# Second attention of a four-stage gated block: scores for the maxima from a stack of their own, and the value products moved into the middle of a step

## The chip, the cores and the metric

The kernel runs on one core of one Trainium2 chip. The metric is the device time of one execution in microseconds (us). A core has five engines that run side by side and wait for one another through semaphores: TensorE (PE; its weight loads are listed apart as PEld), VectorE (DVE), ScalarE (ACT), GpSimd (POOL) and SyncE (SP), which here only issues transfers (DMAs).

## The reference, cut to what matters

Four sublayers are added to x (4 batches, 1024 tokens, 256 channels) one after the other. The change lies in the third, a cross attention of 16 heads of 16 dimensions over 77 context tokens per batch:

```python
def _L1_xattn_ref(values, keys, queries, mask, Wv, Wk, Wq, Wo, bo):
    ...
    energy = jnp.einsum('bqhd,bkhd->bhqk', q, k)
    energy = jnp.where(mask, energy, jnp.float32(-1e+20))
    attn = jax.nn.softmax(energy / np.sqrt(HEAD), axis=-1)
    out = jnp.einsum('bhqk,bkhd->bqhd', attn, v).reshape(N, Lq, EMBED)
    return out @ Wo.T + bo
...
x = x + jnp.tanh(g_xattn[1]) * _L1_xattn_ref(ctx_1024, ctx_1024, _layernorm(x, axis=-1), mask_1x1xSxS2_bk0, ...)
```

x and ctx_1024 are float32. The mask (1024 x 77) is the same for all batches and heads.

## The kernel before, in words

The program is written out by hand: each engine has its own function, the order of its calls is the order of its instructions, and semaphores tie the engines together. The first attention, the expert layer, the second attention and the last attention follow one another; the second attention takes the stretch from 186 to 348 us.

**Operands.** The float32 queries (the normalised x) and keys are split into bfloat16 parts (high, middle, low) and written to memory outside the core (`x_parts`, `ctx_key_parts`). SP loads them back as *stacks*: for one unit, six groups of 16 rows (`Q_ORDER`, `K_ORDER`), so that one bfloat16 matmul over 96 rows adds up the six products of parts. `load_x_stack` (lines 547 to 555) does this with six transfers of 128 KB per unit, each filling 16 partitions that lie next to one another. Three stacks `Xs` are in use in turn; four more rows (96 to 99) take the row maxima. `K1s` is the same for the keys of all heads and batches.

**Units and steps.** A unit u (of 16) is one batch and four heads; a step m (of 32) is half a unit, 512 tokens. `scores1(m)` on PE (line 1456) goes over the four heads j. For each it first makes one *tile* of the next unit for the maxima, `max_product1`: one mask matmul of 308 columns (line 1438, weights `mb1`, moving operand `I4`, four identities side by side) and four matmuls of 77 columns (line 1440), 128 tokens by four heads by 77 keys. Then it makes the transposed scores of its own head, 77 keys by 512 tokens: line 1473 from the stack with the maxima's rows, line 1474 for the mask. In between, in eight of the steps (m = 4, 6, ... 18; the table `HALVES`), ahead of the third head, it transposes a *half* chunk of the normalised x for a later batch (`transpose_half`, line 1394).

After the four heads PE makes `values1(m - 1)` (line 1482), the four transposes of the maxima `max_transposes1(m + 2)` (line 1453) and `out_transposes1(m - 2)` (line 1491):

```python
            for m in range(2 * UNITS):
                scores1(m)
                if m >= 1:
                    values1(m - 1)
                if m + 2 < 2 * UNITS:
                    max_transposes1(m + 2)
                if m >= 2:
                    out_transposes1(m - 2)
```

**The other engines in a step.** DVE takes the maximum of each of the four tiles (line 2054; `max_transposes1(m + 2)` waits for the fourth), in a step with a half also the residue of the half between the second and the third maximum (line 2022), and at the end `normalise1` (lines 2073, 2076). ACT takes the four exponentials (line 1086), in a step with a half the high part of it between the second and the third (`part_h`, line 1028), then `copy_out1` (line 1072) and `stage_rows1` (line 1066). POOL copies the staged maxima into the four rows of the stack (line 833) and makes the low parts (lines 823, 825). Two banks take the tiles in turn, three the scores. ACT's `part_h` waits for the transposes, the residue for `part_h`, the third maximum stands behind the residue.

**Ahead of it.** DVE makes `mb1`, the mask as 0 or minus 2^66 (line 2031). POOL fills `I4` (line 804) and the ones rows of `K1s` (line 808), scales a bias (line 813) and then makes the layer norm's factors (`ln_rstd`, lines 776 and 778).

## Time and profile before

| | |
|---|---|
| median of 3 runs | 1233.62 us (1229.71 to 1234.7) |
| the profiled execution's own time | 1234.39 us |
| its span | 1232.7 us |
| PE busy in the span | 1159.2 us (94%), 10391 matmuls |
| DVE busy | 973.4 us (79%) |
| ACT busy | 818.0 us (66%) |
| POOL busy | 254.9 us (21%) |
| transfers | 40.3% of 16 engines' span, 100 MB |

The span is what the profiler saw from the first instruction to the last; what lies around it is 1.7 us. "Busy" counts the time in which an engine had an instruction under way; matmuls overlap, so a busy PE is not one at its peak. The profile also names what an idle engine waited for, and follows the chain of work that ended last.

### The profile page before, as it was taken

The numbers are of one execution on the slowest core, as the hardware profiler recorded it, in microseconds if no ns is written. First come the engines' busy times: TensorE is split into PE (matmuls) and PEld (weight loads), VectorE is DVE, ScalarE is ACT, GpSimd is POOL, SyncE is SP. The second block draws the span as 40 slices with busy tenths as digits, with TensorE's granted clock in tenths as the row PEclk, the third lists the DMA queues.
The fourth block names the chain that finished last, engine by engine and source line by source line (L and its number), as shares of the span: only waits on it lengthen the run. The fifth ranks groups of instructions, "written<-read, shape, count | busy, mean of one in ns | idle before, by whom it ended". The sixth has DMA issues, their size and how long they took to land.

```text
span 1232.7 us, 26184 instructions
## 1 busy us (share of the span) xinstructions
PE 1159.2 (94%) x10391; PEld 529.1 (43%) x10391; DVE 973.4 (79%) x1431; ACT 818.0 (66%) x1470; POOL 254.9 (21%) x200
## 2 busy tenths in 40 slices
PE   6888999999998999789999999999999999999997
PEld 3566675555575456333332332322323333333345
DVE  6996587765447758789999999999999999999812
ACT  2334567777733742228888888888888888888871
POOL 3021346655732423630000000100100001001010
PEclk9999999999999999979999999999999999999999
DMA  6000337565300334741544354535543545264023
GB/s 207 25 1 16 34 92 140 103 130 107 50 26 26 123 108 137 141 67 47 98 65 87 80 98 74 96 64 102 88 85 74 102 83 87 60 103 76 12 68 117
DMA packets 89993, 101.73 MB, mean 83 GB/s; under 512 B 22154, under 2 KB 60300, under 8 KB 89872
## 3 DMA queue, kind: packets, MB, share of 16 engines
q1 hardware_dynamic: 89872, 100.06, 40.3%
q8 instruction: 83, 1.36, 0.5%
q14 instruction: 38, 0.31, 0.1%
HBM read 71.47 MB, written 24.33 MB: 78 GB/s over the span
## 4 chain that ended last, share of the span: by engine, by line
PE 58%; DVE 34%; ACT 4%; issue 2%; DMA 1%; SPq 1%; POOL 1%; POOLq 0%; DVEq 0%; ACTq 0%
DVE sm L2283 23%; PE ps L1719 11%; PE ps L1710 9%; PE ps L1697 7%; PE ps L1482 3%; PE ps L1579 2%; PE ps L1473 2%; PE ps L1474 2%; PE ps L1780 2%; PE ps L1538 2%; PE ps L1491 1%; PE ps L1440 1%; PE ps L1438 1%; DVE XN L1842 1%; ACT W L1163 1%
## 5 line engine op out<-in xcount | busy, mean ns | idle before, releaser
L2283 DVE TENSOR_REDUCE sm<-ps 128x1 f32<-128x1024 f32 x512 | 602.0, 1219 | 35.2 <-PE ps L1697 31.2
L1163 ACT ACTIVATE W<-ps 128x512 f32<-128x512 f32 x1024 | 535.0, 603 | 122.0 <-PE ps L1719 119.6
L1719 PE MATMUL ps<-R 99*32 99x512 bf16 x4096 | 317.9, 384 | 0.9
L1710 PE MATMUL ps<-W,R 128*32 128x512 f32 x2048 | 265.6, 594 | 0.0
L1719 PEld LDWEIGHTS ps<-R 99*32 99x32 bf16 x4096 | 85.1, 94 | 203.5 <-ACT W L1163 155.9
L1697 PE MATMUL ps<-R 50*128 50x512 bf16 x512 | 91.2, 392 | 12.2 <-DVE sm L2283 8.0
L1697 PE MATMUL ps<-KM,R 50*128 50x512 bf16 x512 | 88.7, 384 | 5.2 <-DVE sm L2283 0.2
L1086 ACT ACTIVATE R<-ps 77x512 f32<-77x512 f32 x128 | 75.2, 593 | 21.0 <-PE ps L1474 11.7
L904 POOL COPY R<-R 128x512 f32<-128x512 f32 x16 | 9.8, 613 | 373.3 <-PE ps L1710 373.3
L1710 PEld LDWEIGHTS ps<-W,R 128*32 128x32 f32 x2048 | 63.0, 111 | 46.1 <-issue 0.9
L833 POOL COPY R<-R 4x2048 bf16<-4x2048 bf16 x32 | 60.5, 1892 | 57.0 <-ACT R L1066 49.0
L2054 DVE TENSOR_REDUCE small<-ps 128x4 bf16<-128x308 f32 x128 | 57.2, 473 | 13.7 <-PE ps L1440 13.7
L1697 PEld LDWEIGHTS ps<-R 50*128 50x128 bf16 x512 | 23.3, 93 | 98.9 <-issue 58.2
L923 POOL TENSOR_TENSOR R<-R,W 128x512 f32<-128x512 f32 x8 | 10.2, 1278 | 265.5 <-DMA W<-sum_factors 265.5
L1697 PEld LDWEIGHTS ps<-KM,R 50*128 50x128 bf16 x512 | 23.3, 93 | 95.8 <-issue 64.9
L1579 PE MATMUL ps<-R,W 128*128 128x512 f32 x128 | 57.9, 595 | 0.0
L1473 PE MATMUL ps<-R 100*77 100x512 bf16 x128 | 49.0, 383 | 0.0
L1474 PE MATMUL ps<-R 77*77 77x512 bf16 x128 | 48.6, 380 | 0.0
L1842 DVE TENSOR_SCALAR XN<-X,mv,rstd 128x256 f32<-128x256 f32 x128 | 47.0, 434 | 1.0 <-PE ps L1551 0.2
L2073 DVE RECIPROCAL small<-ps 128x16 f32<-128x16 f32 x32 | 8.3, 258 | 42.4 <-PE ps L1491 42.4
L1440 PEld LDWEIGHTS ps<-R 96*128 96x128 bf16 x512 | 33.9, 97 | 12.4
L1440 PE MATMUL ps<-R 96*128 96x77 bf16 x512 | 39.0, 198 | 0.0
(261 smaller groups left out, 1451.9 us busy)
## 6 DMA issues: line engine op xcount, KB each, us to landing
R<-x_parts SPq DMA_DIRECT2D x96, 128.0 KB, 4.9
R<-q_parts SPq DMA_DIRECT2D x192, 64.0 KB
R<-q_parts SPq DMA_DIRECT2D x96, 128.0 KB
R<-k_parts SPq DMA_DIRECT2D x96, 128.0 KB
q_parts<-R SPq DMA_DIRECT2D x24, 256.0 KB, 2.6
k_parts<-R SPq DMA_DIRECT2D x24, 256.0 KB, 2.8
x_parts<-R SPq DMA_DIRECT2D x6, 768.0 KB, 4.1
X<-in_x SPq DMA_DIRECT2D x4, 1024.0 KB, 10.0
```

What stands on the lines that cost most here:

```text
L833: pool.tensor_copy(Xs[m // 2 % 3][SR:SR1, :, 512 * (m % 2):512 * (m % 2) + 512], mrow1[:, m % 2].unsqueeze(1).to_broadcast([4, 4, 512])).t ...
L1086: act.activation(P1[:, m % 2, j, :], score_bank1(n)[0:KX, :], ACT.Exp, scale=0.25).then_inc(s_e1, 1)
L1163: act.activation(PR[:, s % 2, h, :], third_bank("score", 64 * u + n), ACT.Exp, scale=0.25).then_inc(s_sfree, 1)
L1440: mm = pe.matmul(o[:, KX * j:KX * j + KX], Xs[u % 3][0:SR, j, P * q:P * q + P], K1s[0:SR, 4 * hg + j, KX * b:KX * b + KX], start=False, st ...
L1473: pe.matmul(o, K1s[:, 4 * hg + j, KX * b:KX * b + KX], Xs[u % 3][:, j, t], start=True, stop=False)
L1474: pe.matmul(o, I4[:, 0:KX], mb1[:, t], start=False, stop=True).then_inc(s_sc, 1)
L1579: mm = pe.matmul(o[:, 512 * j:512 * j + 512], wqkv[:, i, C * kind + P * j:C * kind + P * j + P], XNT3[:, i, 512 * c:512 * c + 512], start= ...
L1697: mm = pe.matmul(pl[:, 512 * i:512 * i + 512], QMH[j][h][v, P * q:P * q + P], KM[j][v, h, :], start=True, stop=True)
L1710: mm = pe.matmul(bank(7)[32 * h:32 * h + 32, :], VST[j][:, k, h, :], PR[:, s % 2, h, :], start=(k == 0), stop=(k == TB - 1))
L1719: mm = pe.matmul(o[32 * c:32 * c + 32, :], KST[j][0:MAX_ROW + 1, h, t:t + 32], QST[j][0:MAX_ROW + 1, h, 512 * (s // 8):512 * (s // 8) + 51 ...
L1842: ins_ = dve.tensor_scalar(ln_chunk_buf(c)[:, i, :], X[:, 4 * c + i, :], mv[:, 4 * c + i, 0:1], rstd[:, 4 * c + i:4 * c + i + 1], ALU.subt ...
L2283: dve.tensor_reduce(MX[:, half, h, q:q + 1], bank(2 * ((p + 1) % 2), 2), AX, ALU.max).then_inc(s_tfree, 1)
```

## The change

The second attention's maxima get their own stack. `max_stack1(u)` has 125 rows: 77 rows of the mask (`mb1`, the same for each head) and 48 rows of parts (`QM_ORDER`, three products of parts in place of six). `max_keys1(b)` stands against it: 77 rows of identity and 48 rows of the keys' parts. A tile is then four matmuls of 77 columns over 125 rows, without the mask matmul. There are two such stacks in turn; their mask rows are filled by POOL (unit 0, which also makes `mb1` now) and by DVE (units 1 and 13), and stay in place. Three more transfers of 128 KB per unit fill the parts. Rows of all these loads are interleaved: transfer n fills every sixth row from n (stacks of the scores, `K1s`) or every third (maxima). `values1(m - 1)` on PE and `copy_out1(m - 1)` on ACT move from the end of step m to between its second and its third head. The order of SP's loads and part writes changes, and POOL fills the identities of three more batches in steps 1, 3 and 4.

```diff
+        MAXR = KX + 48
+
+        def max_stack1(u):
+            v = R5[0:MAXR, 2048:4096] if u % 2 == 0 else R1[0:MAXR, 6144:8192] if u < 12 else R4[0:MAXR, 2048:4096]
+            return v.bitcast(BF16).rearrange("p (j n) -> p j n", j=4)
+
+        def max_keys1(b):
+            v = R2f[0:MAXR, 7482:8098] if b == 0 else W[0:MAXR, 2048 + 616 * b:2664 + 616 * b]
+            return v.bitcast(BF16).rearrange("p (h n) -> p h n", h=H)
...
-        WRITES = {2: (2, 3), 5: (4,), 7: (5,), 9: (6,), 11: (7,)}
+        WRITES = {2: (2,), 5: (4,), 7: (5,), 9: (6,), 11: (7,)}
...
                 for n, p in enumerate(Q_ORDER):
-                    sp.dma_start(Xs[u % 3][16 * n:16 * n + 16],
+                    sp.dma_start(x_stack(u)[n:SR:6],
                                  XP[p, 64 * hg:64 * hg + 64, S * b:S * b + S]
-                                 .rearrange("(j d) t -> d j t", d=D)).then_inc(s_xs[u % 3], 16)
+                                 .rearrange("(j d) t -> d j t", d=D)).then_inc(s_xs[(u + 1) % 3], 16)
+
+            def load_max_stack1(u):
+                b, hg = u // 4, u % 4
+                if u == 2:
+                    sp.wait_ge(s_mp, 8)
+                if u >= 3:
+                    sp.wait_ge(s_sc, 8 * (u - 2))
+                if u == 13:
+                    sp.wait_ge(s_pl, 2 * NC)
+                for n, p in enumerate(QM_ORDER):
+                    sp.dma_start(max_stack1(u)[KX + n:MAXR:3],
+                                 XP[p, 64 * hg:64 * hg + 64, S * b:S * b + S]
+                                 .rearrange("(j d) t -> d j t", d=D)).then_inc(s_xs[u % 3], 16)
...
+            def preset_max_keys1(b):
+                pool.tensor_copy(max_keys1(b)[0:KX], identB[0:KX, 0:KX].unsqueeze(1).to_broadcast([KX, H, KX])
+                                 ).then_inc(s_v1m, 1)
+
+            preset_max_keys1(0)
+            pool.wait_ge(s_m1, 16)
+            pool.tensor_scalar(mb1, M1u, -1.0, BIG, ALU.add, ALU.mult).then_inc(s_mk1, 1)
+            pool.wait_ge(s_mk1, 1)
+            pool.wait_ge(s_kw, 16)
+            pool.tensor_copy(max_stack1(0)[0:KX], mb1.unsqueeze(1).to_broadcast([KX, 4, S])).then_inc(s_mk1, 1)
             pool.wait_ge(s_w1, 16 * 28)
...
+                if m in (1, 3, 4):
+                    pool.wait_ge(s_dl, NC)
+                    preset_max_keys1((m + 1) // 2 if m < 4 else 3)
...
                     if j == 2 and half_in(m) is not None:
                         part_h(half_in(m), bank(2))
+                    if j == 2 and m >= 1:
+                        copy_out1(m - 1)
...
-                if m >= 1:
-                    copy_out1(m - 1)
                 if m + 2 < 2 * UNITS:
                     stage_rows1(m + 2)
...
                     o = bank(n % 2)[:, 0:4 * KX]
-                    pe.matmul(o, mb1[:, P * q:P * q + P], I4, start=True, stop=False, skip_group_check=True)
                     for j in range(4):
-                        mm = pe.matmul(o[:, KX * j:KX * j + KX], Xs[u % 3][0:SR, j, P * q:P * q + P],
-                                       K1s[0:SR, 4 * hg + j, KX * b:KX * b + KX], start=False, stop=True,
+                        mm = pe.matmul(o[:, KX * j:KX * j + KX], max_stack1(u)[:, j, P * q:P * q + P],
+                                       max_keys1(b)[:, 4 * hg + j, :], start=(j == 0), stop=True,
                                        skip_group_check=True)
...
                     n = 4 * m + j
+                    if j == 2 and m >= 1:
+                        values1(m - 1)
                     if j == 2 and half_in(m) is not None:
                         pe.wait_ge(s_mrs, m + 2)
                         transpose_half(half_in(m), bank(2))
...
                 scores1(m)
-                if m >= 1:
-                    values1(m - 1)
...
-            dve.wait_ge(s_m1, 16)
-            dve.tensor_scalar(mb1, M1u, -1.0, BIG, ALU.add, ALU.mult).then_inc(s_mk1, 1)
+
+            def mask_rows1(u):
+                dve.tensor_copy(max_stack1(u)[0:KX], mb1.unsqueeze(1).to_broadcast([KX, 4, S])).then_inc(s_mk1, 1)
...
             for n in range(4, FIRST):
                 residue(n, bank(n))
+            dve.wait_ge(s_dl, NC)
+            dve.wait_ge(s_mk1, 1)
+            mask_rows1(1)
             maxima1(1)
...
+                if m == 19:
+                    dve.wait_ge(s_pl, 2 * NC)
+                    mask_rows1(13)
```

On PE, from the half's transposes of a step to its end (before; L1394 the transposes, L1438 and L1440 a tile, L1473 and L1474 a score, L1482 the values, L1453 the maxima's transposes, L1491 those of the output):

```order
L1394 MATMUL ps<-identF,XN 128x128 x4
L1438 MATMUL ps<-R 128x308
L1440 MATMUL ps<-R 128x77 x4
L1473 MATMUL ps<-R 77x512
L1474 MATMUL ps<-R 77x512
L1438 MATMUL ps<-R 128x308
L1440 MATMUL ps<-R 128x77 x4
L1473 MATMUL ps<-R 77x512
L1474 MATMUL ps<-R 77x512
L1482 MATMUL ps<-R,W 32x512 x4
L1453 MATMUL ps<-identB,small 4x128 x4
L1491 MATMUL ps<-identF,R 128x128 x4
```

The same stretch in the changed program, beginning at the values (L1557 the values, L1463 the half's transposes, L1511 a tile, L1548 and L1549 a score, L1524 and L1566 the transposes at the end):

```order
L1557 MATMUL ps<-R,W 32x512 x4
L1463 MATMUL ps<-identF,XN 128x128 x4
L1511 MATMUL ps<-R 128x77 x4
L1548 MATMUL ps<-R 77x512
L1549 MATMUL ps<-R 77x512
L1511 MATMUL ps<-R 128x77 x4
L1548 MATMUL ps<-R 77x512
L1549 MATMUL ps<-R 77x512
L1524 MATMUL ps<-identB,small 4x128 x4
L1566 MATMUL ps<-identF,R 128x128 x4
L1511 MATMUL ps<-R 128x77 x4
L1548 MATMUL ps<-R 77x512
```

The values stood between the last score and the maxima's transposes and now stand ahead of the half's transposes; nothing is left between the last score and the maxima's transposes, and the mask matmul is gone from the tile.

On ACT in such a step, before (L1086 exponentials, L1028 the half's high part, L1072 the copy of the output, L1066 the maxima's rows):

```order
L1086 ACTIVATE R<-ps 77x512 x2
L1028 CAST R<-ps 128x512
L1086 ACTIVATE R<-ps 77x512 x2
L1072 COPY R<-ps 128x512
L1066 CAST R<-ps 4x512
```

and in the changed program (L1157, L1097, L1141 and L1135 are the same four):

```order
L1157 ACTIVATE R<-ps 77x512 x2
L1097 CAST R<-ps 128x512
L1141 COPY R<-ps 128x512
L1157 ACTIVATE R<-ps 77x512 x2
L1135 CAST R<-ps 4x512
```

The copy of the output moved ahead of the third exponential.

On POOL ahead of the second attention, before (L804 `I4`, L808 rows of `K1s`, L813 the bias, L776 and L778 the layer norm's factors):

```order
L804 COPY R<-identB 77x308
L808 COPY R<-identB 4x1232 x4
L813 TENSOR_SCALAR bo<-bo,gates 128x256
L776 TENSOR_SCALAR rstd<-mv 128x8
L778 TENSOR_TENSOR rstd<-rstd,mhalf 128x8
```

and in the changed program (L865 identities, L870 `mb1`, L873 the mask rows of unit 0, then L876 the bias and L828, L830 the factors):

```order
L856 COPY R<-identB 77x308
L860 COPY R<-identB 4x1232 x4
L865 COPY R<-identB 77x1232
L870 TENSOR_SCALAR R<-R 77x1024
L873 COPY R<-R 77x4096
L876 TENSOR_SCALAR bo<-bo,gates 128x256
L828 TENSOR_SCALAR rstd<-mv 128x8
L830 TENSOR_TENSOR rstd<-rstd,mhalf 128x8
```

Three instructions now stand between the rows of `K1s` and the bias, ahead of the factors.

## Rows read from the trace of the kernel before

**Rows 1.** Chain that ended last, 193 to 341 us, shares by line.

```profile
by line: PE ps L1482 20.2%; PE ps L1473 18.7%; PE ps L1474 18.5%; PE ps L1440 11.6%; PE ps L1491 11.5%; PE ps L1438 11.3%; PE ps L1453 4.9%; PE ps L1394 2.4%; issue 0.7%; DVE small L2054 0.3%
```

**Rows 2.** Steps 0, 1, 16 and 17: stretch; busy us and instructions of PE, PEld, DVE, ACT, POOL; clock; DMA.

```profile
193.34:196.81 3.47, 3.33 (x35) 1.94 (x33) 2.29 (x6) 2.77 (x5) 3.33 (x3) 1.00 0.49 161
196.81:201.00 4.19, 4.19 (x42) 2.11 (x40) 3.73 (x11) 3.21 (x7) 3.67 (x3) 1.00 0.51 172
270.04:275.13 5.09, 5.09 (x50) 3.08 (x48) 2.92 (x7) 4.01 (x8) 3.37 (x3) 1.00 0.88 136
275.13:279.81 4.68, 4.68 (x47) 2.58 (x45) 2.41 (x6) 3.54 (x7) 2.19 (x2) 1.00 0.10 25
```

**Rows 3.** Timeline of step 16, which has a half: start, us, engine, line, operation.

```profile
270.04 0.30 PE L1438 MATMUL ps<-R 77*128 77x308 bf16 x1
...
270.18 0.30 PE L1440 MATMUL ps<-R 96*128 96x77 bf16 x4
...
270.76 0.29 PE L1438 MATMUL ps<-R 77*128 77x308 bf16 x1
...
271.47 0.60 PE L1394 MATMUL ps<-identF,XN 128*128 128x128 f32 x4
...
272.16 0.57 ACT L1028 CAST R<-ps 128x512 bf16<-128x512 f32 x1
...
272.76 0.69 DVE L2022 TENSOR_TENSOR R<-ps,R 128x512 f32<-128x512 f32 x1 [1.03 <-ACT R L1028]
...
273.37 0.85 DVE L2054 TENSOR_REDUCE small<-ps 128x4 bf16<-128x308 f32 x2
...
273.42 1.07 PE L1482 MATMUL ps<-R,W 77*32 77x512 f32 x8
...
274.28 0.24 PEld L1453 LDWEIGHTS ps<-identB,small 128*4 128x4 bf16 x4 [0.70 <-DVE small L2054]
274.32 0.39 PE L1453 MATMUL ps<-identB,small 128*4 128x128 bf16 x4
```

**Rows 4.** Timeline, end of step 0, which has no values behind its scores.

```profile
195.62 0.30 PE L1440 MATMUL ps<-R 96*128 96x77 bf16 x4
...
195.96 0.48 DVE L2054 TENSOR_REDUCE small<-ps 128x4 bf16<-128x308 f32 x1 [0.23 <-PE ps L1440]
...
196.49 0.39 PE L1453 MATMUL ps<-identB,small 128*4 128x128 bf16 x4
...
196.81 0.30 PE L1438 MATMUL ps<-R 77*128 77x308 bf16 x1
```

**Rows 5.** POOL's timeline ahead of the second attention, and the copies of line 833.

```profile
139.17 5.92 POOL L808 COPY R<-identB 4x1232 bf16<-4x1232 bf16 x4
145.19 2.03 POOL L813 TENSOR_SCALAR bo<-bo,gates 128x256 f32<-128x256 f32 x1
154.39 1.60 POOL L776 TENSOR_SCALAR rstd<-mv 128x8 f32<-128x8 f32 x1 [7.17 <-DVE mv L2008]
...
L833 POOL COPY R<-R 4x2048 bf16<-4x2048 bf16 x32 | 60.5, 1892 | 57.0 <-ACT R L1066 49.0 <-POOL R L825 3.0 <-POOL R L833 2.7
```

**Rows 6.** DVE: a copy of 3072 elements; last maxima ahead of step 0, transposes that follow.

```profile
L1954 DVE CAST R<-small 128x3072 bf16<-128x3072 f32 x1 | 1.8, 1760 | 0.0
...
191.02 0.85 DVE L2054 TENSOR_REDUCE small<-ps 128x4 bf16<-128x308 f32 x2
...
193.03 0.39 PE L1453 MATMUL ps<-identB,small 128*4 128x128 bf16 x4 [0.65 <-DVE small L2054]
```

**Rows 7.** Timeline, the first tile of step 14.

```profile
260.29 0.29 PE L1438 MATMUL ps<-R 77*128 77x308 bf16 x1 [0.93 <-issue]
```

**Rows 8.** Two stretches of loads: columns as in rows 2, last two DMA share and GB/s.

```profile
4.00:16.00 12.00, 5.93 (x11) 3.62 (x12) 6.69 (x33) 0.83 (x2) 2.02 (x3) 1.00 1.09 354
255.00:260.00 5.00, 4.36 (x39) 2.15 (x37) 4.01 (x11) 3.67 (x7) 1.97 (x2) 1.00 0.97 123
```

**Rows 9.** Timeline, the last values, and what they waited for.

```profile
343.48 1.07 PE L1482 MATMUL ps<-R,W 77*32 77x512 f32 x8 [0.21 <-ACT R L1072]
```

More of the change, by code:

```diff
@@ L222, in build_program, with x_stack @@
         xres = R4[:, 2048:4096].rearrange("p (u j n) -> p u j n", u=2, j=2)
-        Xs = [v.bitcast(BF16).rearrange("p (j n) -> p j n", j=4)
-              for v in (R4[0:SR1, 0:2048], R5[0:SR1, 0:2048], R5[0:SR1, 2048:4096])]
+        QM_ORDER, KM_ORDER = (0, 0, 1), (0, 1, 0)
+        def x_stack(u):
+            v = (R4[0:SR1, 0:2048], R5[0:SR1, 0:2048], R1[0:SR1, 4096:6144] if u == 2 else R2f[0:SR1, 0:2048])[u % 3]
+            return v.bitcast(BF16).rearrange("p (j n) -> p j n", j=4)
+        MAXR = KX + 48
+        def max_stack1(u):
+            v = R5[0:MAXR, 2048:4096] if u % 2 == 0 else R1[0:MAXR, 6144:8192] if u < 12 else R4[0:MAXR, 2048:4096]
+            return v.bitcast(BF16).rearrange("p (j n) -> p j n", j=4)
+        def max_keys1(b):
+            v = R2f[0:MAXR, 7482:8098] if b == 0 else W[0:MAXR, 2048 + 616 * b:2664 + 616 * b]
+            return v.bitcast(BF16).rearrange("p (h n) -> p h n", h=H)
         On = R1[:, :].rearrange("p (i c) -> p i c", i=NT)
@@ L264, in build_program, with group_loads @@
         s_x3 = sem("x3_added")
-        STACK_DMAS = 6
+        STACK_DMAS, MAX_DMAS = 6, 3
+        def group_loads(g):
+            return 16 * sum((MAX_DMAS if n < UNITS else 0) + (STACK_DMAS if n else 0) for n in range(g % 3, g + 1, 3))
         FIRST = 8
@@ L538, in _, with load_max_keys1 @@
             sp.dma_start(M1u, ins["mask1T"]).then_inc(s_m1, 16)
+            def load_max_keys1(b):
+                for n, p in enumerate(KM_ORDER):
+                    sp.dma_start(max_keys1(b)[KX + n:MAXR:3],
+                                 KXP[p].rearrange("(h d) n -> d h n", d=D)[:, :, KX * b:KX * b + KX]
+                                 ).then_inc(s_k1s, 16)
+            load_max_keys1(0)
             for n, p in enumerate(K_ORDER):
-                sp.dma_start(K1s[16 * n:16 * n + 16],
+                sp.dma_start(K1s[n:SR:6],
                              KXP[p].rearrange("(h d) n -> d h n", d=D)).then_inc(s_k1s, 16)
@@ L564, in _ @@
             sp.wait_ge(s_kw, 48)
+            load_max_stack1(0)
             load_x_stack(0)
+            sp.wait_ge(s_dl, NC)
+            load_max_stack1(1)
             sp.wait_ge(s_pl, 4)
@@ L573, in _ @@
                     sp.wait_ge(s_pw[1], 16 * (b + 1))
+                if u >= 2:
+                    load_max_stack1(u)
+                if u == 3:
+                    write_parts(3)
                 load_x_stack(u)
+                if u == 3:
+                    sp.wait_ge(s_k1s, 16 * (MAX_DMAS + STACK_DMAS))
+                    for n in range(1, B):
+                        load_max_keys1(n)
                 for c in WRITES.get(u, ()):
@@ L832, in max_rows1 @@
                     pool.wait_ge(s_sc, 4 * (m - 5))
-                pool.tensor_copy(Xs[m // 2 % 3][SR:SR1, :, 512 * (m % 2):512 * (m % 2) + 512],
+                if m == 10:
+                    for n in range(2):
+                        pool.wait_ge(s_pw[n], 32)
+                pool.tensor_copy(x_stack(m // 2)[SR:SR1, :, 512 * (m % 2):512 * (m % 2) + 512],
                                  mrow1[:, m % 2].unsqueeze(1).to_broadcast([4, 4, 512])).then_inc(s_mrc, 1)
@@ L1424, in _ @@
             keep_warm(3, 4)
-            pe.wait_ge(s_k1s, 16 * STACK_DMAS)
-            pe.wait_ge(s_v1m, 8)
-            pe.wait_ge(s_mk1, 1)
+            pe.wait_ge(s_k1s, 16 * (MAX_DMAS + STACK_DMAS))
+            pe.wait_ge(s_v1m, 9)
             pe.wait_ge(s_v1c, 2)
@@ L1431, in max_product1 @@
                 b, hg = u // 4, u % 4
-                pe.wait_ge(s_xs[u % 3], 16 * STACK_DMAS * (u // 3 + 1))
+                pe.wait_ge(s_xs[u % 3], group_loads(u))
+                pe.wait_ge(s_mk1, 4 if u >= 13 else 3 if u >= 1 else 2)
+                if b >= 1:
+                    pe.wait_ge(s_k1s, 16 * (MAX_DMAS * B + STACK_DMAS))
+                    pe.wait_ge(s_v1m, 9 + b)
                 for q in qs:
@@ L1471, in scores1 @@
                     t = slice(512 * q, 512 * q + 512)
-                    pe.matmul(o, K1s[:, 4 * hg + j, KX * b:KX * b + KX], Xs[u % 3][:, j, t], start=True, stop=False)
+                    pe.matmul(o, K1s[:, 4 * hg + j, KX * b:KX * b + KX], x_stack(u)[:, j, t], start=True, stop=False)
                     pe.matmul(o, I4[:, 0:KX], mb1[:, t], start=False, stop=True).then_inc(s_sc, 1)
```

4 lines of the change are left out of this document (3 added, 1 removed).

## The prediction, made before the changed kernel had run

> **What bounds the kernel now.** I read the chain of waits first, over the 148 us of the second attention: nearly all of it is PE, and the mask matmuls (L1438) alone hold 11.3% of it [rows 1]. The windows by step then show PE busy for the whole of a step: 4.68 us in a plain step, 5.09 us in one with a half [rows 2]. So a matmul taken off PE can shorten a step, as long as nothing else is nearly as late. That second limit is read from two timelines.
>
> In step 16 [rows 3] two heads take 1.43 us (270.04 to 271.47), 0.715 each, and the mask matmul is 0.14 of it (270.04 to 270.18), 0.13 where it is not rounded up. From the maxima's transposes to the next step it is 0.81 us (274.32 to 275.13). The plain step is then 4 x 0.715 + 0.81 + the values, so the values cost 1.01 us, and a half's transposes 5.09 - 4.68 = 0.41 us.
>
> The second reading is how late the maxima's transposes may start. They wait for DVE's fourth maximum. Step 0 has no values after its scores, and there this wait shows: from the fourth tile's first 77 column matmul to the transposes it takes 0.87 us (195.62 to 196.49), with the maximum running in between, and 0.32 more to the next step [rows 4]. PE's own work in that time is less: 0.14 + 0.43 = 0.57 us. In all later steps the values stand there and cover the wait. In a step with a half the path is longer: transposes of the half, ACT's high part, DVE's residue, third and fourth maximum, maxima's transposes: 271.47 to 274.28, 2.81 us, and the values end within 0.04 us of it [rows 3]. That chain has no slack even before the change.
>
> **The change, part by part.** All against the profiled execution, 1234.39 us (span 1232.7).
>
> 1. *Mask matmul gone.* 0.13 us per tile, 0.52 per step if PE stays the limit. The stack's 125 rows in place of 96 cost nothing here: the mask matmul over 77 rows and the score over 100 rows take their columns' time alike. A head then costs 0.585 us.
>
> 2. *Values between second and third head.* They no longer cover the maxima. Plain step: the fourth tile starts at 3 x 0.585 + 1.01 = 2.77 us, the transposes 0.87 later, the next step 0.81 later: 4.45 us, against 4.68. The gain is 0.23, not 0.52. Step with a half: its transposes now start after the values, at 2 x 0.585 + 1.01 = 2.18 us instead of 1.43, and the same 2.81 and 0.81 follow: 5.80 us, against 5.09. **It gets 0.71 us longer.** ACT does not change this: E2 and E3 wait behind `part_h` and the copy, but end before the values of the next step need them. POOL is busy for 3.37 of 5.09 us and has room. Steps 2 to 29 hold 20 plain ones (-4.6 us) and 8 with a half (+5.7). Step 0 loses its 3.47 - 0.52; step 1, 4.19 now, becomes 2.77 + 0.87 + 0.32 = 3.96: together -0.8. Sum of the loop: +0.3.
>
> 3. *POOL ahead of the loop.* It gets a copy of 1232 elements, the mask of 1024 and a copy of 4096. By line 808 (5.92 us for four of 1232, so 1.5 each) and line 833 (1.89 us for 2048) these are 1.5, about 2 (the bias' 256 elements took 2.03, so this is loosely known) and 3.8: 7.3 us [rows 5]. POOL is free from 147.2 us until the factors at 154.39, so 0.1 us would be late; at line 808's rate the last copy takes 4.9 us. I take +0.7, with 0 and +4 as ends. Nothing covers it, since PE stands idle until the normalised x comes.
>
> 4. *DVE's mask rows.* A copy of 4096 bfloat16 elements. The nearest row is a copy of 3072 in 1.76 us, so 2.35 us [rows 6]; the ends are 1.2 (twice that rate) and 4.3 (about the rate of a maximum over a bank). The first stands ahead of the maxima that started at 191.02. Those took 2.0 us to the transposes at 193.03, of which 0.25 was waiting for PE's warm matmuls. So +2.1 us. The second, in step 19, ends 1.5 us into the next step, normalise and first maximum follow, and the third tile waits: +0.6 us.
>
> [...]
>
> 5. *Loads.* Nine transfers per unit instead of six. The maxima's stack is now loaded on its own and first, and the scores' stack is needed a unit later. Before, step 14 waited 0.93 us for the first load of batch 2 [rows 7]: I count -0.9. The queue took 0.97 of the engines for 123 GB/s in those loads, while 128 partition loads ran at 354 GB/s [rows 8]. Interleaved rows should lie nearer the second, and I charge nothing for the three more.
>
> [...] No run so far shows interleaved rows here.
>
> 6. *End.* The last values waited for a copy that now comes before them: 0.4 us at 343.48, where PE waited on ACT [rows 9], and 0.2 us in the two steps without maxima: -0.6. The first tiles ahead of the loop are ready sooner: -0.1. The three identity copies in steps 1, 3 and 4 (1.5 us each) lie in POOL's idle time.
>
> Sum: 0.3 + 0.7 + 2.1 + 0.6 - 0.9 - 0.6 - 0.1 = **+2.1 us**, 1236.5 for that execution. The median of the runs shown is 0.8 us lower, so the forecast is **1235.7 us**: no change. A measurement of this kernel can tell 0.5%, 6.2 us, from none: below 1227.5 is faster, above 1239.8 slower.
>
> **Rivals.**
>
> *The maxima are not exposed* (DVE starts or ends earlier than I think, or the half's chain does): then steps fall to PE's own sum, 4.16 and 4.57 us. 20 x -0.52 and 8 x -0.52 in place of -4.6 and +5.7 make the result 15.7 us lower, 1220. PE's full occupation speaks for it, step 0 against it. Chance 0.15.
>
> *Half of that*: plain steps as forecast, but the half's chain is shortened (the high part may begin as soon as the first half's transposes are out): half steps stay at 5.1, the result is 5.7 lower, 1230. Chance 0.15.
>
> *Loads become the limit.* The interleaving gives nothing: a unit's 1152 KB at 123 GB/s are 9.4 us, and 384 KB of parts written 1.1 at the rate of the wide load, 10.5 together, against 10.25 for a unit (4.45 + 5.80). It decides from the moment a unit's loads take longer than its two steps, first at step 14, where the part of a batch is written just before. 0.3 us for each of 12 units and about a microsecond at each of three batches: +6, 1242. The 0.97 share at 123 GB/s speaks for it, the wide load's 354 against it. Chance 0.12.
>
> *The copies are slow.* POOL's 4 us and DVE's 4.3 us twice: +3.3, +2, +2: 1243. It decides once POOL ends after 154.39. Chance 0.1; POOL's 2.03 us for 256 elements speaks for it.
>
> **How the numbers follow.** The forecast as computed has 0.48 and lies between 1232 and 1240. Range: 1226 to 1243; it leaves out most of the first rival and the upper tails, two in ten. Faster: the first rival and a quarter of the second, 0.2. Slower: both last rivals where they pass 1239.8 (0.17) and the edge of the forecast, 0.23. The same: 0.57.
>
> **What would show it.** In the changed trace: a plain step of 4.45 us with PE idle for some 0.3 us ahead of the maxima's transposes, released by the maximum; a half step of 5.8 us with over a microsecond there; no wait at step 14; POOL's factors after 154.4 us; the last maxima ahead of step 0 about 2 us later. Steps of 4.2 and 4.6 us would make it wrong on the fast side; a wait for a load at a unit's first tile on the slow side.

## The result, and the profile after

| | before | changed |
|---|---|---|
| median | 1232.8 us (1229.71 to 1234.7, 4 runs) | 1247.34 us (1242.86 to 1251.2, 4 runs) |
| profiled execution | 1234.39 us, span 1232.7 | 1247.35 us, span 1245.6 |

The changed kernel takes 1.0112 times as long, 95% interval 1.0084 to 1.0139: slower, and above the forecast's range (1226 to 1243). PE makes fewer matmuls (10263, 10391 before), but is busy for as long: 1161.1 us, 1159.2 before. The page of the changed kernel, busy us (share of the span) and instructions:

```profile
PE 1161.1 (93%) x10263; PEld 521.8 (42%) x10263; DVE 977.5 (78%) x1432; ACT 814.1 (65%) x1470; POOL 264.3 (21%) x206
```

Where the 13 us of the two profiled executions lie is read by distances between five marks, the same instructions in both timelines: POOL's first copy for the second attention, DVE's first normalised x, the first and the second of the maxima's transposes, and the last. Timelines of the changed kernel at these marks:

```profile
141.20 0.44 POOL L856 COPY R<-identB 77x308 bf16<-77x308 bf16 x1 [10.37 <-PE ps L1457]
...
163.19 2.67 DVE L1915 TENSOR_SCALAR XN<-X,mv,rstd 128x256 f32<-128x256 f32 x8
...
196.48 0.39 PE L1524 MATMUL ps<-identB,small 128*4 128x128 bf16 x4 [0.57 <-DVE small L2129]
...
202.38 0.58 PE L1524 MATMUL ps<-identB,small 128*4 128x128 bf16 x4 [0.65 <-DVE small L2129]
...
349.87 0.38 PE L1524 MATMUL ps<-identB,small 128*4 128x128 bf16 x4
```

| stretch | before | changed | difference |
|---|---|---|---|
| start to POOL's first copy | 138.67 | 141.20 | +2.5 |
| to the normalised x | 19.11 | 21.99 | +2.9 |
| to the first transposes | 30.99 | 33.29 | +2.3 |
| to the second transposes | 4.26 | 5.89 | +1.6 |
| to the last transposes (loop) | 142.49 | 147.49 | +5.0 |
| to the end | 897.16 | 895.77 | -1.4 |

The last row lies behind the change: over all profiles below that stretch took 894.0 to 899.1 us, so its -1.4 tells nothing.

The steps first. The windows of steps 16 (with a half) and 17 in the changed kernel, columns as in [rows 2]:

```profile
284.25:290.15 5.90, 4.90 (x47) 2.60 (x45) 2.91 (x7) 3.84 (x8) 3.33 (x3) 1.00 0.71 159
290.15:294.69 4.54, 4.41 (x42) 2.12 (x40) 2.41 (x6) 3.35 (x7) 2.22 (x2) 1.00 0.17 59
```

A step with a half went from 5.09 to 5.90 us, a plain one from 4.68 to 4.55 [rows 2]. In the half step PE is idle for a full microsecond. The timeline of step 16 in the changed kernel shows where:

```profile
284.24 0.31 PE L1511 MATMUL ps<-W,R 125*128 125x77 bf16 x4
...
284.83 0.31 PE L1511 MATMUL ps<-W,R 125*128 125x77 bf16 x4
...
285.51 1.06 PE L1557 MATMUL ps<-R,W 77*32 77x512 f32 x8
...
286.51 0.66 PE L1463 MATMUL ps<-identF,XN 128*128 128x128 f32 x4
...
287.20 0.59 ACT L1097 CAST R<-ps 128x512 bf16<-128x512 f32 x1 [0.99 <-PE ps L1463]
...
287.82 0.69 DVE L2095 TENSOR_TENSOR R<-ps,R 128x512 f32<-128x512 f32 x1 [1.89 <-ACT R L1097]
...
288.43 0.85 DVE L2129 TENSOR_REDUCE small<-ps 128x4 bf16<-128x308 f32 x2
...
289.33 0.39 PE L1524 MATMUL ps<-identB,small 128*4 128x128 bf16 x4 [1.00 <-DVE small L2129]
```

The values (L1557) stand ahead of the half's transposes (L1463); from there the chain of ACT, DVE and two maxima takes 289.33 - 286.51 = 2.82 us, as before [rows 3]. It starts later in the step by what the values take. A head takes 0.59 us (284.24 to 284.83).

The two stretches ahead of the loop are DVE's and POOL's. Timelines of the changed kernel, DVE and POOL from 147 to 160 us:

```profile
145.31 1.22 DVE L2067 TENSOR_TENSOR R<-R 128x1024 f32<-128x1024 f32 x1 [3.45 <-ACT R L1083]
147.66 2.30 DVE L2072 SCALAR_TENSOR_TENSOR X<-R,gates,X 128x1024 f32<-128x1024 f32 x1 [1.12 <-ACT R L1087]
149.88 2.05 DVE L2067 TENSOR_TENSOR R<-R 128x1024 f32<-128x1024 f32 x1
153.06 3.41 DVE L2072 SCALAR_TENSOR_TENSOR X<-R,gates,X 128x1024 f32<-128x1024 f32 x1 [1.12 <-ACT R L1087]
...
161.99 1.28 DVE L2072 SCALAR_TENSOR_TENSOR X<-R,gates,X 128x1024 f32<-128x1024 f32 x1 [1.12 <-ACT R L1087]
```

```profile
147.67 1.21 POOL L865 COPY R<-identB 77x1232 bf16<-77x1232 bf16 x1
148.97 1.90 POOL L870 TENSOR_SCALAR R<-R 77x1024 bf16<-77x1024 uint8 x1
150.93 4.46 POOL L873 COPY R<-R 77x4096 bf16<-77x4096 bf16 x1
155.38 1.89 POOL L876 TENSOR_SCALAR bo<-bo,gates 128x256 f32<-128x256 f32 x1
159.91 1.06 POOL L828 TENSOR_SCALAR rstd<-mv 128x8 f32<-128x8 f32 x1 [2.65 <-DVE mv L2081]
```

POOL's own lateness cost nothing: it waited 2.65 us for DVE before the factors. But DVE's operation at L2072 takes 1.28 us alone and 2.30 and 3.41 us beside POOL's copies. The excess is about what is left of POOL's copy when DVE starts: 155.39 - 153.06 = 2.33 us are left, 3.41 - 1.28 = 2.13 came on top. That the copy is the cause, and not only the neighbour in time, is what an experiment below tests.

PE then has nothing to do, and its granted clock falls. Windows of the changed kernel, columns as above:

```profile
160.00:170.00 10.00, 5.34 (x21) 4.53 (x21) 7.75 (x14) 6.06 (x9) 2.64 (x2) 0.72 0.00 0
...
200.00:210.00 10.00, 8.24 (x56) 4.21 (x60) 6.35 (x15) 4.43 (x8) 8.04 (x6) 0.66 0.50 138
```

A mean granted clock of 0.72 and 0.66 means that part of each stretch ran at a lower clock: by windows of 2 us it was 1.00 from 160 to 164 and 0.50 from 166 to 170 us, 0.97 from 200 to 202 and 0.50 from 202 to 208. The timeline shows the idle PE ahead of it, and what runs slowly then (PE and DVE):

```profile
164.72 4.02 PE L1463 MATMUL ps<-identF,XN 128*128 128x128 f32 x16 [4.54 <-DVE XN L1915]
...
198.74 1.84 DVE L2105 COPY R<-R 77x4096 bf16<-77x4096 bf16 x1
...
201.11 0.62 PE L1511 MATMUL ps<-R 125*128 125x77 bf16 x8 [1.90 <-DVE small L2129]
...
205.36 0.63 PE L1548 MATMUL ps<-R 100*77 100x512 bf16 x1
```

The copy L2105 stands ahead of the second maxima, PE waits 1.90 us for them, and a score matmul takes 0.63 us in step 0, where in later steps it takes 0.38. Step 0 took 5.08 us, 3.47 before [rows 2], and forecast at 2.95.

### The profile page after: what moved, and what is told of

Its sections match the earlier page's. It is cut to its first block, busy times and chain, and to the rows that moved or that the text cites. A ratio compares the mean times of both kernels' runs of the same rounds, so it can differ in the third digit from the quotient of the medians.

```text
span 1245.6 us, 26125 instructions
## 1 busy us (share of the span) xinstructions
PE 1161.1 (93%) x10263; PEld 521.8 (42%) x10263; DVE 977.5 (78%) x1432; ACT 814.1 (65%) x1470; POOL 264.3 (21%) x206
## 4 chain that ended last, share of the span: by engine, by line
PE 56%; DVE 35%; ACT 4%; issue 2%; DMA 1%; SPq 1%; POOL 0%; POOLq 0%; DVEq 0%; ACTq 0%
DVE sm L2364 23%; PE ps L1792 11%; PE ps L1783 9%; PE ps L1770 7%; PE ps L1557 3%; PE ps L1652 3%; PE ps L1853 2%; PE ps L1611 2%; PE ps L1548 2%; PE ps L1549 2%; PE ps L1511 2%; DVE small L2129 2%; PE ps L1566 1%; DVE XN L1915 1%; ACT W L1232 1%
## 5 line engine op out<-in xcount | busy, mean ns | idle before, releaser
L1157 ACT ACTIVATE R<-ps 77x512 f32<-77x512 f32 x128 | 72.7, 593 | 20.8 <-PE ps L1549 19.1
L1548 PE MATMUL ps<-R 100*77 100x512 bf16 x128 | 50.0, 390 | 0.0
L1549 PE MATMUL ps<-R 77*77 77x512 bf16 x128 | 49.6, 388 | 0.0
L1020 ACT COPY R<-ps 128x1024 f32<-128x1024 f32 x16 | 15.7, 1014 | 35.0 <-PE ps L1298 35.0
L1511 PEld LDWEIGHTS ps<-W,R 125*128 125x128 bf16 x384 | 24.6, 98 | 25.3 <-issue 14.3
L1557 PE MATMUL ps<-R,W 77*32 77x512 f32 x256 | 34.1, 605 | 0.3 <-ACT R L1157 0.3
```

The costliest lines, as they stand in the source:

```text
L1157: act.activation(P1[:, m % 2, j, :], score_bank1(n)[0:KX, :], ACT.Exp, scale=0.25).then_inc(s_e1, 1)
L1548: pe.matmul(o, K1s[:, 4 * hg + j, KX * b:KX * b + KX], x_stack(u)[:, j, t], start=True, stop=False)
L1549: pe.matmul(o, I4[:, 0:KX], mb1[:, t], start=False, stop=True).then_inc(s_sc, 1)
L1557: mm = pe.matmul(bank(7)[32 * j:32 * j + 32, :], V1a[:, u // 4, 4 * (u % 4) + j, :], P1[:, m % 2, j, :], start=True, stop=True)
```

## The experiments

The distances of every profiled kernel, worked out as above (us; "loop" is from the second to the last transposes), and the median of its runs. The experiments were measured in three sessions; the kernel before had medians of 1233.3 to 1234.4 us in them:

| kernel | first copy at | x | 1st | 2nd | loop | median |
|---|---|---|---|---|---|---|
| before | 138.67 | 19.11 | 30.99 | 4.26 | 142.49 | 1232.8 |
| before_again | 138.89 | 19.10 | 30.98 | 4.26 | 142.18 | 1235.48 (one) |
| changed | 141.20 | 21.99 | 33.29 | 5.89 | 147.49 | 1247.34 |
| after_again | 142.58 | 21.99 | 32.92 | 5.89 | 154.64 | 1247.63 |
| e1_values_back | 141.36 | 21.99 | 31.62 | 5.90 | 136.23 | 1233.51 |
| e2_half_first | 138.75 | 21.99 | 33.29 | 5.89 | 140.79 | 1238.13 (one) |
| e3_contiguous | 139.15 | 21.99 | 31.77 | 5.89 | 154.04 | 1248.76 |
| e4_warm | 141.26 | 21.99 | 30.74 | 6.43 | 145.27 | 1242.64 |
| e5_pool_late | 140.63 | 19.00 | 37.29 | 5.83 | 145.08 | 1243.57 (one) |
| e6_copy_early | 137.14 | 21.99 | 33.29 | 4.13 | 145.35 | 1239.56 (one) |
| e8_normalise_third | 140.69 | 21.99 | 31.68 | 5.90 | 135.17 | 1234.21 |
| e7_best | 135.65 | 19.10 | 35.42 | 6.43 | 135.49 | 1231.43 |
| e9_best | 140.59 | 20.15 | 32.41 | 4.13 | 128.48 | 1222.61 |

### Both kernels again

> The changed kernel once more, unedited. Its profiled run was 12.96 us longer than that of the kernel before (1247.35 against 1234.39), and 2.5 us of that lie ahead of the copy with which the second attention's preparation begins (POOL's identity copy, 138.67 against 141.20), where the program is unchanged. If those 2.5 us are run-to-run, this copy starts within 1 us of 138.7 here, and the time is nearer 1245; if the change causes them, it starts at 141 again. From that copy on, both theories expect what the first profile showed: 22.0 us to the normalised x, 33.3 to the first maxima's transposes, 5.9 to the second, plain steps of 4.55 us and half steps of 5.9.

> The kernel before once more, for a second profile. The profiled runs so far start the second attention's preparation anywhere from 135.65 to 142.58 us, with the same program ahead of it. If that is run-to-run and not the change, the kernel before also starts it elsewhere than at its 138.67 this time, while the distances behind it stay: +19.1 us to the normalised x, +31.0 to the first maxima's transposes, +4.3 to the second, 142.5 for the loop, each within 0.3 us. If the distances move as well, by a microsecond or more, the ledger by distances is no better than the whole time.

Between the two profiles of each kernel the distances repeat to 0.4 us, except for after_again's loop. They hide a spread that the table shows: after_again, e1_values_back, e2_half_first, e3_contiguous and e8_normalise_third keep the order of instructions ahead of the loop on DVE, POOL and PE, and their distance to the first transposes lies anywhere from 31.62 to 33.29 us. The changed kernel's +2.3 is the upper end of +0.6 to +2.3. The first copy starts anywhere from 135.65 to 142.58 us in kernels whose programs ahead of it are alike, so the 2.5 us of the first row of the ledger may be run-to-run; the two profiles of before (138.67, 138.89) do not bound it. That loop is 7.2 us longer, all of it in steps 1 to 3 (7.07, 7.06 and 6.27 us against 4.59, 4.07 and 4.55), where the lower clock (0.50) held from 202.5 to 226.4 us; in the first profile it held from 201.9 to 208.7. Windows of after_again:

```profile
208.00:215.00 7.00, 7.00 (x38) 2.56 (x36) 3.12 (x9) 3.47 (x7) 2.96 (x2) 0.50 0.65 202
215.00:222.00 7.00, 7.00 (x37) 2.56 (x36) 3.59 (x17) 3.48 (x7) 4.89 (x4) 0.50 0.68 190
```

So what a stall of PE ahead of step 0 costs was not the same in each run. Steps 0 to 3 together took 18.3 us in the changed kernel's profile, 25.5 in after_again and 24.4 in e3_contiguous, and 15.8 in e5_pool_late, whose clock stayed at 1.00 (below).

### Values back at the end of a step

```diff
-                    if j == 2 and m >= 1:
-                        values1(m - 1)
...
                 scores1(m)
+                if m >= 1:
+                    values1(m - 1)
```

and the same for `copy_out1` on ACT.

> The changed kernel with the values and their copy back at the end of a step. Theory: between the second and third score the values push the half's transposes back by 1.0 us and leave DVE's last maximum uncovered; at the end of the step they cover it. Then a plain step is 4 x 0.585 + 1.01 + 0.81 = 4.16 us (4.55 in the changed kernel), a half step 1.17 + 2.81 + 0.81 = 4.79 (5.9): 20 x 0.39 + 8 x 1.1 = 16.6 us less, some 0.5 given back at the end where the last values wait for their copy: 1231 us, a little below the kernel before. Rival: DVE sets the step wherever the values stand (four maxima, normalise, residue), so that steps stay at 4.5 and 5.5 or more: less than 5 us gained, 1242 or more. What happens ahead of the loop stays as in the changed kernel by both.

Half steps took 4.80 us (4.79 forecast), plain ones 4.42 to 4.43 (4.16). The loop is 11.3 us shorter and the median, 1233.51, is that of before (ratio 1.001, interval 0.9983 to 1.0036). 9.2 of the 11.3 us lie in the steps from 4 on, which ran at a granted clock of 1.00 in both. Step 0, which has no values in either kernel, is 1.0 shorter (4.13, 5.08) by the clock, which fell only in the middle of it here (0.52 from 202 to 204 us). Step 6 took 6.35 us, where it was 5.94: PE was idle for 1.40 us ahead of the first tile of unit 4. Even so the place of the values is the largest single cause. The windows of e1_values_back, steps 16 and 17, and the timeline of a plain step's tiles and DVE:

```profile
274.83:279.63 4.80, 4.76 (x46) 2.68 (x44) 2.91 (x7) 4.08 (x9) 3.32 (x3) 1.00 0.83 183
279.63:284.06 4.43, 4.32 (x43) 2.22 (x41) 2.41 (x6) 3.29 (x6) 2.23 (x2) 1.00 0.31 76
```

```profile
270.90 0.42 DVE L2151 TENSOR_TENSOR R<-ps,small 128x256 f32<-128x256 f32 x1
271.00 0.31 PE L1511 MATMUL ps<-W,R 125*128 125x77 bf16 x4
...
271.24 2.03 DVE L2129 TENSOR_REDUCE small<-ps 128x4 bf16<-128x308 f32 x4
...
271.83 0.20 PEld L1511 LDWEIGHTS ps<-W,R 125*128 125x128 bf16 x4 [0.56 <-issue]
```

The third tile comes at 271.83 where 271.00 + 0.59 = 271.59 was due: it needs the bank of the first, and DVE's maximum of that one stands behind the normalise.

### The half ahead of the values

```diff
-                    if j == 2 and m >= 1:
-                        values1(m - 1)
                     if j == 2 and half_in(m) is not None:
                         pe.wait_ge(s_mrs, m + 2)
                         transpose_half(half_in(m), bank(2))
+                    if j == 2 and m >= 1:
+                        values1(m - 1)
```

> The changed kernel with the half's four transposes ahead of the values at the third score, instead of behind them. Theory: the half's chain (transposes, high part, residue, two maxima, maxima's transposes) takes 2.81 us from its first transpose; it starts 1.01 us sooner, so a half step is 1.17 + 2.81 + 0.81 = 4.79 us where it was 5.9, plain steps stay at 4.55: 8 x 1.1 = 9 us less than the changed kernel, 1238. The score banks of heads two and three then wait for the values, which end at 1.17 + 0.41 + 1.01 = 2.59 us; the fourth tile starts at 3.2 and its transposes 0.87 later are at 4.05, so 4.87 by that second path: both give 4.8 to 4.9. Rival: the half is not what makes these steps long, the third and fourth tile are late behind the values anyway: 5.5 us or more, 3 us gained at most.

Half steps took 4.99 to 5.00 us (4.8 to 4.9 forecast; 5.55 in step 6), plain ones still 4.55, and the loop was 6.7 us shorter, where 9 had been forecast. It is one run, at 1238.13 us. The order of the half and the values is what made most of these steps' length.

### Warming matmuls, and DVE's copy earlier

e4_warm raises `keep_warm` by 12 matmuls ahead of step 0 and adds 20 ahead of the first transposes of the normalised x; e6_copy_early moves `mask_rows1(1)` on DVE to behind `ln_chunks(2, [2])`. In the changed kernel the granted clock was 0.72 from 160 to 170 us, behind 4.54 us of idle PE, and 0.66 from 200 to 210 us, behind 1.90.

> The changed kernel with 20 more warming matmuls while PE waits for the normalised x, and 12 more while it waits for the maxima ahead of step 0. [...] With PE kept busy the clock stays at 1.0 in both: 2 us less between the normalised x and the maxima's transposes, 1 to 2 less in steps 0 and 1: 1243.5 to 1244.5. Rival: the work there is bound by DVE and ACT, not by PE's speed, and the lower clock costs nothing: the same time within 1 us, or up to 1 us more where the warming itself delays the first transposes.

> The changed kernel with DVE's mask copy for unit 1 (1.8 us) moved from between the first and the second four maxima to a place 15 us earlier, where DVE waits for ACT. Theory: ahead of the second maxima nothing covers it. So the second maxima's transposes come 1.6 us sooner after the first (4.3 instead of 5.9 us), PE does not stand idle for 1.9 us in step 0, its granted clock there is 1.0 instead of 0.66, and step 0 is 3.0 us as forecast instead of 5.1: 3.5 us less in all, 1244. Rival: the copy has taken the place of a wait that is there anyway (for the stack's loads or for the normalised x), so the two distances stay within 0.5 us, and what is gained in one is lost in the other.

Windows of e4_warm, and then of e6_copy_early:

```profile
160.00:170.00 10.00, 9.23 (x51) 5.98 (x49) 7.75 (x14) 6.01 (x9) 2.70 (x2) 1.00 0.01 2
200.00:210.00 10.00, 9.25 (x88) 4.24 (x88) 7.90 (x27) 8.14 (x14) 7.73 (x6) 1.00 0.68 207
```

```profile
160.00:170.00 10.00, 9.23 (x36) 7.97 (x37) 8.88 (x17) 6.10 (x10) 2.26 (x2) 0.66 0.00 0
200.00:210.00 10.00, 9.44 (x88) 4.34 (x88) 6.92 (x26) 7.84 (x15) 9.10 (x7) 1.00 0.82 245
```

With matmuls in the gap the granted clock stays at 1.00 in both windows and the first transposes come 2.55 us sooner, though the normalised x is as late as in the changed kernel; step 0 is 2.97 us, as the forecast had it (2.95). The median is 4.7 us below the changed kernel's. The early copy does the same for step 0 without any warming, since there is no gap: second transposes 4.13, step 0 2.97, by the distances 3.9 us less. (Its one run is 7.8 us below the changed kernel's median; 4.1 of that lie ahead of the first copy, at 137.14.) Both theories hold, on the clock and on the copy: the clock did not fall ahead of step 0 in any of the four profiles without the gap (e4, e6, e7, e9: 1.00 from 198 to 212 us), and it fell in six of the seven with it (to 0.50 to 0.52 by windows of 2 us). The seventh comes next.

### POOL's copies elsewhere

```diff
             ln_rstd(2, [1])
             pool.wait_ge(s_rs, 2 * (2 * B + 2))
+            preset_max_keys1(0)
...
             max_rows1(0)
```

(the three operations of POOL from the identity to the mask copy).

> The changed kernel with POOL's key identity, bias and mask copy of the first stack (1.2, 1.9 and 4.5 us) moved behind its second set of factors, where POOL has nothing to do. Theory: these three slow DVE's operations beside them (from 1.2 and 1.3 us to 2.05, 2.3 and 3.4), and through DVE the normalised x, which then comes 2.9 us later than before the change. Moved away, DVE's four operations take 1.2 to 1.3 us again and the normalised x comes at +19.1 us from the start of POOL's copies (22.0 in the changed kernel); the first maxima's transposes are about 5 us earlier, as PE does not stand idle and its clock stays up: 1242. It may give back a microsecond where the copy now lies beside other DVE work. Rival: POOL's own lateness held up the factors, or the operations are slow for another reason (the loads of the stacks, which write the same memory then): the DVE durations stay as they are and the time at 1246 to 1248. What is left out of neither: all of the computation is done.

The normalised x came at +19.00 us, the 2.9 us are gone. But the first transposes are 4.0 us later. DVE's and POOL's timelines of e5_pool_late:

```profile
180.74 5.43 DVE L1915 TENSOR_SCALAR XN<-X,mv,rstd 128x256 f32<-128x256 f32 x4
181.78 3.59 POOL L908 COPY R<-R 77x4096 bf16<-77x4096 bf16 x1
```

Four pieces of the normalised x, 1.37 us elsewhere, now took 5.43: the copy stopped DVE here as well, and I had moved it onto another DVE operation that PE waits for. So the theory of the cause stands; "about 5 us earlier" was wrong.

DVE's copy stayed ahead of the second maxima here, so PE's wait ahead of step 0 did too. PE's timeline, and the window of step 0:

```profile
201.49 0.61 PE L1511 MATMUL ps<-R 125*128 125x77 bf16 x8 [1.83 <-DVE small L2129]
...
202.75:205.72 2.97, 2.84 (x28) 1.58 (x28) 1.96 (x5) 2.43 (x5) 2.28 (x2) 1.00 0.50 137
```

PE was idle for 1.83 us, and the granted clock stayed at 1.00. A wait of that length need not lower it; what decided it is not shown.

### Neighbouring rows again

```diff
-                sp.dma_start(K1s[n:SR:6],
+                sp.dma_start(K1s[16 * n:16 * n + 16],
```

and so for the three other stacks.

> The changed kernel with all its stack loads to 16 neighbouring rows again, as in the kernel before. Theory: interleaving makes each load land sooner (3.3 us from issue, 4.9 with neighbouring rows before the change), but in the changed kernel nothing waits for a load in the loop, so with neighbouring rows nine loads a unit keep the queue busy for longer and it is just hidden: the loop within 1 us of 147.5, or some 2 us longer where a batch's first unit is loaded late. Rival: the queue at neighbouring rows is full (a unit's 1152 KB at 123 GB/s are 9.4 us of 10.5), so waits for loads stand at most units' first tiles: the loop 5 us or more longer, 1252.

The steps are the same: 4.55 and 5.90, no wait at step 14; the loop of 154.04 is that of after_again, with the same three steps at the lower clock (0.50 from 200.5 to 220.5 us). The transfers differ much. DMA issues (KB each, median us to landing), changed kernel and e3_contiguous:

```profile
R<-x_parts SPq DMA_DIRECT2D x144, 128.0 KB, 3.3
```

```profile
R<-x_parts SPq DMA_DIRECT2D x144, 128.0 KB, 6.1
```

and the windows of 125 us of each, DMA share and GB/s last:

```profile
215.00:340.00 125.00, 114.75 (x1038) 57.12 (x1037) 73.50 (x192) 89.13 (x159) 78.63 (x52) 1.00 0.59 156
```

```profile
215.00:340.00 125.00, 114.66 (x1010) 56.94 (x1009) 71.83 (x187) 87.26 (x156) 74.35 (x47) 0.98 0.99 147
```

Interleaving takes the engines' share from 0.99 to 0.59 for the same bytes. Here it buys no time (1248.76 us against 1247.34), since both were hidden.

### Normalise behind the second maximum, and all together

> The kernel with the values back at the end of a step, and with DVE's normalise of the previous step between its second and third maximum instead of ahead of the first. In that kernel a plain step took 4.42 us where the parts of PE add up to 4.16. Theory: the normalise (0.26 + 0.42 us with its wait) ahead of the first maximum holds up the third tile by 0.27 us, since that tile takes the bank of the first. Behind the second maximum it fits into DVE's slack: plain steps 4.16 us, half steps unchanged at 4.8: 20 x 0.26 = 5 us less, 1228.5. Rival: PE's own queue or its weights set the 4.42 (the third score's tile waits as part of issue), and the step stays at 4.4: 1233.5.

> All that the other experiments point to, in one kernel, on the changed kernel: the values at the end of a step, the normalise behind the second maximum, the half's transposes at the second head, the bias by DVE as before the change, POOL's copies behind its second factors, DVE's copy 15 us earlier, the warming matmuls. Theory, against the changed kernel's ledger: 2.9 us for the normalised x, 2.5 for the lower clock behind it, 1.6 ahead of the second maxima, 2.1 in step 0, plain steps of 4.16 us (20 x 0.39), half steps of 4.6 (8 x 1.3), 0.5 given back at the end: 27 us less, 1220. Rival: at the shorter steps another resource takes over (the loads of a unit, POOL's rows, ACT), and the steps stay at 4.4 and 4.8 or a wait for a load stands at a unit's start: 1228 or more.

In both, plain steps took 4.15 to 4.16 us, so the third tile's wait was the normalise. The time did not follow. e8 took 1234.21 us, no different from e1_values_back, where 1228.5 was forecast; e7 took 1231.43, where 1220 was forecast (0.9973 of the kernel before, interval 0.9957 to 0.9988). Three things stood in the way: 6.5 us (e8) and 8.4 (e7) in step 6, where PE waited for the stack of unit 4, behind nine loads of key rows in SP's queue; 5.10 us in each of three steps, where POOL's addition of a bias makes its rows late; and in e7 POOL's copy, met by DVE as in e5 (L2066 at 174.24 took 4.67 us beside it, 1.21 at 182.46). The first was there in e1 already (6.35 us). In e7 the clock fell too behind the wait of 2.08 us, to a mean of 0.78 from 221.5 to 229.3 us. And e8's profile lost another 1.6 us in step 1 (5.50 us, 3.88 in e1), most of it at the lower clock (0.50 from 202 to 208 us). The timelines of e7_best and of e8_normalise_third:

```profile
211.10 6.31 SPq L562 DMA_DIRECT2D W<-ctx_key_parts  x9
...
223.95 0.40 PE L1510 MATMUL ps<-W,R 125*128 125x77 bf16 x4 [2.08 <-DMA R<-x_parts]
```

```profile
298.71 4.54 POOL L933 TENSOR_TENSOR X<-X,bo 128x2048 f32<-128x2048 f32 x1
303.31 3.84 POOL L899 COPY R<-R 4x2048 bf16<-4x2048 bf16 x2
...
305.26 0.32 PE L1511 MATMUL ps<-W,R 125*128 125x77 bf16 x4 [0.77 <-POOL R L899]
```

The half's transposes at the second head (e7) gave nothing: 4.84 us against 4.80. e9_best takes these three away:

```diff
-                if u == 3:
-                    sp.wait_ge(s_k1s, 16 * (MAX_DMAS + STACK_DMAS))
-                    for n in range(1, B):
-                        load_max_keys1(n)
+                if u in (1, 5, 6):
+                    n = {1: 1, 5: 2, 6: 3}[u]
+                    sp.wait_ge(s_k1s, 16 * (MAX_DMAS * n + STACK_DMAS))
+                    load_max_keys1(n)
...
+            for j in range(4):
+                if j == 2:
+                    add_zero_factor(0)
+                dve.tensor_copy(max_stack1(0)[0:KX, j], mb1).then_inc(s_mk1, 1)
```

The other edits are those that its expectation names.

> On the changed kernel: values at the end of a step and normalise behind the second maximum, as in the last two; POOL's three operations ahead of the loop done by DVE instead, in two gaps where it waits for ACT (3.45 and 1.12 us; identity 0.6, bias 0.7, mask in four pieces of 0.45); DVE's copy for unit 1 in a gap 15 us earlier; the three batches' key rows loaded at units 1, 5 and 6 instead of all at unit 3, where they stood in the queue ahead of unit 4's stack; POOL's addition of a bias (4.5 us, at four places in the loop, 0.95 us late each) in two halves; no warming. Theory: normalised x at +19.1 us, first maxima's transposes 31.0, second 4.1, steps 0 to 2 about 3.0, 4.0 and 3.9, plain steps 4.16, half steps 4.8, no wait for a load: a loop of 29 steps of some 128 us: against the kernel before 14 us less, 1220. Rival: the written parts of a batch set when the next batch's first unit can be loaded (they wait for the half steps), so shorter steps give back in a wait at units 4, 8 and 12 what they gain: 1228 or more.

It ran in 1222.61 us (1220 forecast), 0.9915 of the kernel before (interval 0.9885 to 0.9945): faster than both, than the kernel before by a little under 1%. The windows of steps 16 and 17:

```profile
267.11:271.91 4.80, 4.76 (x47) 2.68 (x45) 3.01 (x7) 4.08 (x9) 3.33 (x3) 1.00 0.83 171
271.91:276.06 4.15, 4.15 (x43) 2.29 (x41) 2.32 (x6) 3.28 (x6) 2.23 (x2) 1.00 0.34 85
```

The loop is 14.0 us shorter than before the change, and no step waits for a load. The part ahead of it (20.15 + 32.41 + 4.13) is 2.3 us longer than before the change: DVE's small operations in the gap ran beside POOL's copies (7.07 us, 5.91 elsewhere) and took longer than I had counted: identity 1.47 for 0.6, mask 1.70 for 0.7, the first two copies 1.65 for 0.9. So the normalised x came at 20.15. PE stood idle for 2.32 us ahead of its transposes, and the clock fell there again (0.90 and 0.76 from 160 to 170 us).

## Why the prediction was wrong

**The forecast was +2.1 us; the two profiled executions differ by 13.** Two steps of it failed: that POOL's copies cost nothing beside DVE's work (+0.7 forecast, +5.2 in this profile with the clock behind it), and that the clock stays up in steps 0 and 1 (-0.8 forecast, +2.0). A third term, the length of a step, was sized 0.10 us too short. Point by point:

*Mask matmul gone.* Right: a head of 0.585 us, 0.59 measured.

*Steps.* The mechanism was right, and the 0.71 us by which a half step gets longer is what e1 and e2 confirm. Both kinds came out 0.10 us above the forecast: 4.55 and 5.90 against 4.45 and 5.80. It lies behind the values: from their start to PE's next work it is 1.00 us (285.51 to 286.51), and was 0.90 where the maxima's transposes followed them (273.42 to 274.32, [rows 3]). The 0.10 in front of them (285.51, where 284.24 + 2 x 0.585 = 285.41 was due) was there before the change and is in the 1.01 that I had for the values. Why the next work starts later is not shown. The term that was mis-sized is small, but counts in 28 steps: 2.8 us.

*Steps 0 and 1.* Forecast -0.8, measured (5.08 + 4.59) - (3.47 + 4.19) = +2.0. **This step failed: I took the clock as given.** 2.95 us is right at a granted clock of 1.00 (2.97 in e4, e5 and e6), but behind the wait that I had priced myself in front of it the clock fell, in this profile and in five of the six others that have the wait.

*POOL ahead.* **This is the step that failed by the most.** I asked whether POOL would be late (+0.7), and took its copies for work that lies beside DVE's for nothing. POOL was not late; DVE was stopped while POOL copied. Measured +2.9 for the normalised x, and +2.3 behind it because PE stood idle for 4.54 us and its clock fell (e4, with PE kept busy, takes the 2.3 away by itself). The 2.9 repeats in every profile with POOL's copies in this place; the 2.3 is 0.6 to 2.3. The end of +4 that I gave the term was for another mechanism and not wide enough for 5.2.

How far they stopped each other can be read from the changed kernel's timelines. Had L2072 at 153.06 done its work only after POOL's copy had ended, it would have ended at 155.39 + 1.28 = 156.67 us; it ended at 156.47. For L2067 at 149.88, beside L870, that is 150.87 + 1.22 = 152.09; it ended at 151.93. Both fit to 0.2 us. With the 2.9 us measured here in place of my 0.7 the forecast would have been 1238, before the clock. One row does not fit: L2067 at 145.31 took its usual 1.22 us beside copies of line 860, over four partitions. What sets which operations stop each other is not shown.

*DVE's mask rows.* +2.1 forecast for the first, +1.6 measured: the copy takes 1.84 us, not 2.35, beside a copy of POOL's, and 1.21 in e6, where POOL was idle. The second, in step 19, cost nothing (4.55 us), forecast +0.6.

*Loads.* The wait at step 14 is gone, as forecast. It is not the interleaving that did it: with neighbouring rows it is gone too (5.90 in e3). The stack of its own, asked for in another order, is enough.

*End.* -0.6 forecast; from the last transposes to the last values it is -0.1 (8.44 to 8.34).

Of the rivals, unexposed maxima (1220) and half of that (1230) are refuted by the steps, loads as the limit by e3. "The copies are slow" came nearest to the time (1243), but its condition, POOL past 154.39, was met (157.27 less the 2.5 us of the later start is 154.7) without the effect I tied to it.

What stays open: how much of the 2.5 us ahead of the first copy belongs to the change, and what sets whether the clock falls behind a short wait of PE and for how long (until 208.7 us in one profile, until 226.4 in another, not at all in e5). What is settled: the values' place gives back 11.3 us in the loop (e1, about 1 of it the clock's in step 0), POOL's copies 2.9 (e5, which lost it again elsewhere), the clock behind them 2.6 (e4), DVE's copy with the clock in step 0 3.9 (e6: 1.76 + 2.14). That is some 20 us, with the clock's 1 us counted once, against the 13 lost. The other 7 are mostly what the saved mask matmul gives once the values cover the maxima again: in e1 a plain step takes 4.43 us against 4.68 before the change, a half step 4.80 against 5.09, 20 x 0.25 + 8 x 0.29 = 7.3.

## What to carry to other kernels

A matmul that is saved on a full engine is worth what the next limit leaves of it: before moving work into the middle of a step, ask which wait it covered where it stood. "Beside other work" was not free for POOL next to DVE (2.13 us on top of an operation of 1.28); look for the DVE operation that each POOL copy will meet. And price a stall of PE twice: the wait, and, as a range from nothing upwards, the work behind it at the lower clock (granted 0.50 for 0 to 23.9 us behind a wait of 1.8 to 1.9 here).
